# Per-head exponentials with the negated maximum as bias, in place of a subtraction pass, in the two 16-head attentions of an eight-layer kernel

## The reference

```python
# layer A
attn = jnp.einsum('bhqd,bhkd->bhqk', qh * scale, kh)
m = jnp.max(attn, axis=-1, keepdims=True)
e = jnp.exp(attn - m)
attn = e / (jnp.exp(-m) * 0 + 1.0 + jnp.sum(e, axis=-1, keepdims=True))
x = jnp.einsum('bhqk,bhkd->bhqd', attn, vh)
...
# layer G
attn = jnp.einsum('bhqd,bhkd->bhqk', q, k) * scale + bias   # bias: (1, 16, 1024, 77)
attn = jnp.where(mask, -jnp.inf, attn)
probs = jax.nn.softmax(attn, axis=-1)
```

## Time and profile before

| | |
|---|---|
| median of 3 runs | 1860.37 us (1858.97 to 1861.12) |
| the profiled execution | 1866.39 us, of which the span is 1864.4 us |
| mean granted TensorE clock in it | 0.894 of full speed |
| layer A's loop | about 54 to 224 us of the span |
| layer G's loop | about 1212 to 1412 us of the span |
| busy share of the span | TensorE 84%, VectorE 49%, ScalarE 28%, GpSimd 3% |

### The profile page before, as it was taken

How to read it: one execution, slowest core, us unless ns; L and a number is a source line. 1 busy time by engine, 2 the same in 40 slices (tenths; PEclk the granted TensorE clock), 3 DMA queues, 4 the chain that set the end, 5 groups by cost and what they waited for, 6 DMA issues and landing times.

```text
span 1864.4 us, 24953 instructions
## 1 busy us (share of the span) xinstructions
PE 1565.2 (84%) x9284; PEld 1040.6 (56%) x9284; DVE 904.6 (49%) x2156; ACT 521.6 (28%) x1133; POOL 55.3 (3%) x70
## 2 busy tenths in 40 slices
PE   2588799856998887999878899688885599999998
PEld 1466588743565465667667788455554343434343
DVE  4577722376575597242533434478882422222222
ACT  1243433312475361230411244232321111111111
POOL 0700000000001000000010000000000000000000
PEclk8799899967999899898957999889995699999999
DMA  8000000000000100000050000011100000000000
GB/s 331 1 0 0 1 0 0 1 0 1 1 2 1 46 2 1 0 1 0 3 193 1 0 0 0 1 28 27 27 1 0 1 0 12 0 11 0 11 0 11
DMA packets 25083, 33.30 MB, mean 18 GB/s; under 512 B 17621, under 2 KB 22607, under 8 KB 23871
## 3 DMA queue, kind: packets, MB, share of 16 engines
q1 hardware_dynamic: 25023, 32.49, 5.3%
HBM read 30.37 MB, written 2.11 MB: 17 GB/s over the span
## 4 chain that ended last, share of the span: by engine, by line
PE 62%; DVE 17%; issue 12%; ACT 5%; DVEq 1%; DMA 1%; POOL 0%; SPq 0%; ACTq 0%; POOLq 0%
PE ps L2162 12%; PE ps L2171 6%; PE ps L1187 4%; PE ps L669 3%; PE ps L682 3%; PE ps L317 2%; DVE work L504 2%; PE ps L291 2%; PE ps L1650 2%; PE ps L1985 2%; DVE work L505 2%; PE ps L304 1%; PE ps L331 1%; PE ps L2164 1%; PE ps L1996 1%
## 5 line engine op out<-in xcount | busy, mean ns | idle before, releaser
L2162 PE MATMUL ps<-hall,big 128*128 x512 | 237.7, 609 | 6.7 <-DVE x L2266 5.1
L2261 DVE TENSOR_TENSOR work<-work,ps 128x512 f32<-128x512 f32 x64 | 44.1, 688 | 275.9 <-ACT work L2198 275.9
L2162 PEld LDWEIGHTS ps<-hall,big 128*128 128x128 f32 x512 | 99.4, 196 | 130.9 <-issue 130.9
L2198 ACT ACTIVATE work<-ps 128x512 f32<-128x512 f32 x64 | 38.2, 597 | 339.9 <-PE ps L2164 339.9
L2171 PE MATMUL ps<-work,big 128*128 128x512 f32 x256 | 127.0, 619 | 0.9 <-DVE work L2262 0.9
L331 PE MATMUL ps<-work,hall 78*32 78x128 f32 (+1 forms) x2048 | 72.2, 283 | 33.6 <-ACT work L399 29.2
L317 PE MATMUL ps<-pack_const,work 128*78 128x128 f32 (+1 forms) x512 | 78.2, 302 | 25.2 <-ACT work L390 22.6
L304 PE MATMUL ps<-hall,work 128*128 128x308 f32 x256 | 89.9, 455 | 2.2 <-DVE work L478 2.2
L399 ACT COPY work<-ps 78x1024 f32<-78x1024 f32 (+1 forms) x64 | 64.2, 1004 | 80.5 <-PE ps L317 80.5
L317 PEld LDWEIGHTS ps<-pack_const,work 128*78 128x78 f32 (+1 forms) x512 | 60.7, 147 | 42.4 <-ACT work L390 29.9
L331 PEld LDWEIGHTS ps<-work,hall 78*32 78x32 f32 (+1 forms) x2048 | 54.1, 112 | 54.2 <-ACT work L399 42.4
(11 more groups left out here) (436 smaller groups left out, 2712.0 us busy)
## 6 DMA issues: line engine op xcount, KB each, us to landing
big<-in_w SPq DMA_DIRECT2D x3, 2048.0 KB, 15.3
dpack<-in_fside SPq DMA_DIRECT2D x8, 616.0 KB, 4.6
dpack<-in_pack_D SPq DMA_DIRECT2D x1, 4115.0 KB, 18.5
big<-in_pack_B SPq DMA_DIRECT2D x1, 2052.0 KB, 13.8
pack_F<-in_pack_F SPq DMA_DIRECT2D x1, 2052.0 KB, 25.6
x<-in_x SPq DMA_DIRECT2D x1, 2048.0 KB, 8.4
out<-x SPq DMA_DIRECT2D x4, 512.0 KB, 2.9
pack_E<-in_pack_E SPq DMA_DIRECT2D x1, 1027.0 KB, 21.5
```

The source lines that it names most:

```text
L2162: mm = nc.tensor.matmul(ps[:, bank + e % 2, :], MB[name][:, e, c, :], xnT_tok[:, c, bass.ds(i * BLK, BLK)], start=c == 0, stop=c == DC - 1)
L2261: link(ve.tensor_tensor(a, MW["sg"][:, e % 2, :], ps[:, 2 + e % 2, :], ALU.mult))
```

## The change

In both layers VectorE no longer subtracts. It takes the maximum with its sign turned (`negate=True`) and raises `sub_ready` on that, without the `link`. ScalarE takes the exponentials of a unit in 8 instructions of 77 columns, one for each head, with that head's negated maximum as a per-partition bias; in `A` it reads the scores straight from PSUM, in `G` from `sub`, which holds scores plus bias. The 8-column exponential in `A` now has scale 1 in place of -1. Because `A`'s scores stay in PSUM until the exponentials have read them, TensorE's `scores(i, u)` for `u >= 2` waits in `A` for `p_ready` of unit `u - 2` in place of its `sub_ready`. The sums still come from the product with ones.

```diff
@@ heads16_pe, scores @@
                 if u >= 2:
-                    pe.wait_ge(s("sub_ready"), nth(i, NU, u - 2) + done(L, "sub_ready"))
+                    held = "p_ready" if L == "A" else "sub_ready"
+                    pe.wait_ge(s(held), nth(i, NU, u - 2) + done(L, held))
@@ heads16_act, exps @@
                 sub = A["sub"][:, u % 2, :].rearrange("p (h s) -> p h s", h=HPC)
+
+                def powers():
+                    for h in range(HPC):
+                        v = s_psum(u)[:, h // 4, h % 4, :] if L == "A" else sub[:, h, :]
+                        a = nc.scalar.activation(p[:, h, 0:SC], v, ACT.Exp, bias=A["mx"][:, u % 2, h:h + 1])
+                    return a
+
                 if L == "A":
                     nc.scalar.activation(A["em"][:, u, :], A["mx"][:, u % 2, :], ACT.Exp,
-                                         scale=-1.0).then_inc(s("em_ready"), 1)
-                    nc.scalar.activation(p[:, :, 0:SC], sub, ACT.Exp).then_inc(s("em_ready"), 1)
+                                         scale=1.0).then_inc(s("em_ready"), 1)
+                    powers().then_inc(s("em_ready"), 1)
                     act.wait_ge(s("em_ready"), nth(i, 2 * NU, 2 * u + 1))
                     nc.scalar.activation(p[:, :, SC], A["em"][:, u, :], ACT.Copy, scale=0.0, bias=1.0).then_inc(s("p_ready"), 1)
                 else:
-                    nc.scalar.activation(p, sub, ACT.Exp).then_inc(s("p_ready"), 1)
+                    powers().then_inc(s("p_ready"), 1)
@@ heads16_dve, shift @@
-                link(ve.tensor_reduce(m.rearrange("p (k h) -> p k h", k=2), src, AX.X, ALU.max))
-                ve.tensor_tensor(quad(A["sub"][:, u % 2, :]), src,
-                                 m.rearrange("p (k h o) -> p k h o", k=2, o=1).to_broadcast([P, 2, 4, SC]),
-                                 ALU.subtract).then_inc(s("sub_ready"), 1)
+                ve.tensor_reduce(m.rearrange("p (k h) -> p k h", k=2), src, AX.X, ALU.max, negate=True).then_inc(s("sub_ready"), 1)
```

More of the change, by code:

```diff
@@ L553, in heads16_dve @@
             if L == "A":
-                per = 1 + 4 * 1 + 4 * 1 + 2 * 2
+                per = 1 + 4 * 1 + 2 * 2
                 with dve.Fori(0, HT - 1) as i:
@@ L560, in heads16_dve @@
             else:
-                per = 2 * (1 + 3 * 2 + 1 + 4 * 2 + 2 * 2)
+                per = 2 * (1 + 3 * 1 + 4 * 2 + 2 * 2)
                 with dve.Fori(0, HT // 2 - 1) as i:
```

## The result

The changed kernel takes 1885.67 us (median of 4 runs, 1881.77 to 1889.81), the kernel before 1859.67 us in the same comparison (1857.51 to 1861.12). The ratio is 1.0141, 95% interval 1.0113 to 1.0169: slower, by 26 us. The forecast was 1876, range 1865 to 1892. The profiled execution took 1882.94 us, with a span of 1880.9 us, a little under the median of its four, while the profiled execution of before (1866.39 us) was longer than any of the four of this comparison. The two spans differ by 16.5 us only; the medians say 26.

What follows compares the result with a forecast made beforehand. VectorE was late and ScalarE idle before the exponentials; with the change ScalarE becomes the limit in A. A's +17.9 us and G's -2 made +16 on 1860.4, forecast 1876 us, range 1865 to 1892.

Steps and rivals of the forecast that it cites:

- The new wait of `scores`: In A, TensorE's wait on `p_ready` of `u - 2`: costed at nothing, as the turning ahead waits for the same signal.
- Stage A's chain: Per pair of A, four serial bursts of 1.84 us move `weigh_v(2)` from 12.13 to 14.64: +2.51 us, +17.9 in all.
- The first pair: In A, VectorE's held `normed` covers what units 0 to 2 lose; only unit 3's burst counts, +0.3 us.
- Stage G's burst: In G, eight exponentials of 77 columns at a step of 0.217 us take 1.84 us, as in A.
- G's term: Per pair of G, `weigh_v(2)` comes at 13.94, not 14.27: a gain of 0.33 us, taken as -2 in all.
- the sentence that counted the source at nothing: PSUM (A) or SBUF (G) as the exponentials' source makes no difference: 0.70 and 0.72 us against 0.687.
- the sum: Whole kernel: 17.9 in A less 2 in G, +16 us on the median of 1860.4, giving 1876 us.
- rivals 2 and 3: TensorE's clock falls in A: 1888 us, chance 0.10; or stops falling in G: 1864 to 1866 us, chance 0.09.
- signs of being wrong: Step outside 0.18 to 0.26, A's granted clock falling, or ScalarE in A still waiting for VectorE at units 1 to 3.
- the argument that none was as long as G's: Against clock falls in A: its four pauses a pair, 0.7 to 1.5 us, are all shorter than G's 2.08.
- Rival 4: Short exponentials nearly free at 0.12 us each, burst 1.1; G gains 1.8 a pair, about 1846 us, chance 0.05.

Runs made afterwards that it cites:

- g_psum: The changed kernel, but in G VectorE writes scores plus bias back to PSUM and the exponentials read PSUM there; 1882.89 us, ratio 1.0115.

## Why the prediction was right, and where it was not

**The direction and the place** were right: the loss is A's, by four bursts on ScalarE with nothing between them, and VectorE's saved pass is used at unit 0 alone. The new wait of `scores` cost nothing: the timeline shows no stop at L305 that the turning ahead of it had not.

**Stage A's chain** was right in size. Forecast 14.64 for `weigh_v(2)`, measured 14.50; the burst 1.84 against 1.82, the step 0.217 against 0.212. The pair grew by 2.38 where 2.51 was forecast. The first pair did not grow: 31.86 us before and after, where +0.3 was taken.

**Stage G's burst was mis-sized, and the sign of G's term with it.** The step that failed is the sentence that counted the source at nothing. Both rows that I drew the line through have PSUM as their source, and G reads SBUF: 0.250 in place of 0.217, a burst of 2.10 in place of 1.84. Three bursts on the chain make 3 x 0.26 = 0.8 of the 0.89 by which `weigh_v(2)` came late. G's pair grew by 0.5 in place of shrinking by 0.33, over 8 pairs +4 us where -2 was taken. `g_psum` shows it: with the other source the forecast of 13.94 is met within 0.03, and so are the steps to it: unit 3's bias starts at 9.54 (forecast 9.50) and its exponentials at 11.22 (forecast 11.16). The prediction had weighed the source by 0.70 and 0.72 against 0.687 us, a difference of 0.01 to 0.03 an instruction, and called it less than could be told; on a chain of 21 steps the measured 0.038 is 0.8 us. The estimate from the Trainium skill's page "ScalarE: Activation LUTs" (section "What ACT_TABLE_LOAD costs") was 251 ns for the step and 344 for the last one. This is what G shows, 0.250 and 0.347 us, and I had set it aside for A's figure in both layers.

**The clock** was in the rivals and not in the sum, and rivals 2 and 3 both came about in part. One of the prediction's own signs of being wrong is thereby met: A's granted clock fell, to 0.91 over the stretch shown. A's clock fell in 3 of 5 pairs (1.7 us each, as priced) though no pause in A is longer than 1.5 us, so the argument that none was as long as G's was not enough. G's fell in 1 of 6 in place of 5. In the profiled executions these two nearly cancel. That the sum came within 10 us of the measured time with both of them in play is luck: nothing in the prediction set one against the other. How often the clock falls is not given by the pause alone: `g_psum` has 1.92 and five falls, the changed kernel 1.90 and one. The kernels with a filled pause show that the falls go with it; what decides in which pair the clock falls is open.

**The sum.** Without the clock the change costs 19 to 23 us; the forecast chains gave 16, by 17.9 and -2, the measured ones 7 x 2.38 = 17 and 4. The remaining 3 to 7 us of the 26 are the clock's and the scatter's: the kernel before spread over 1853 to 1870 us in the later comparisons, and the interval of the ratio goes from 21 to 31 us. The split of that part was not settled.

**Rival 4** (short exponentials nearly free) was wrong for this kernel because of the bias operand: without it the step from PSUM is the 0.120 that the rival had, the step from SBUF 0.158, and the time is 1841 us in one run, where the forecast of that rival had been 1846.

## What to carry to other kernels

Count a per-partition bias by the instruction, not by the pass: eight short activations with one cost 0.09 us each over eight without, and that was what made the trade a loss. Take the price of an operation from a row with the same source memory. A pass moved from a late engine to an idle one pays only at the unit where the first engine's lateness is on the path and the second has room before its next work. Of the five units that were changed alone (0 and 1 in A, 1, 2 and 3 in G) unit 2 of G gave 0.8 us a pair and unit 1 of G 0.2, the others lost, and changing unit 2 alone beat changing all.

## What the runs showed that was not expected

- An exponential of 77 columns steps by 0.120 us from PSUM and by 0.158 from SBUF; a per-partition bias adds 0.092 to both.
- Seven products of identity tiles in a pause of 1.65 us keep TensorE at full clock (22.0 to 22.2 us a pair, no fall in the six from the second on), where without them three of six pairs took 23.4 to 23.8 us.
- A fall can last twice as long, as in G's second pair of before (pause 2.08 us, pair 26.05 us): with a pause of 2.36 us three pairs took 26.3 us and the others 24.5 to 24.9, against 23.2 at full clock.
